# Turning the next batch's split queries and keys by DMA instead of on TensorE, and starting batch 1's attention inside round 0

## What is computed

```python
x = x + rnn(x, cond);  x = x + lstm(x, cond)        # both a scan over the tokens
x = x + hyperbolic_transformer(x, cond)
x = x + mixture_of_experts(x, cond)

# hyperbolic_transformer
xm = expmap0(layer_norm(logmap0(x)) * (1 + sc) + sh)
q, k, v = (to_heads(plin(xm, w, b)) for w, b in ...)        # 16 heads of 16
attn = softmax(logmap0(q) @ logmap0(k).T / 4);  o = expmap0(attn @ logmap0(v))
x1 = mobius_add(x, expmap0(g * logmap0(plin(from_heads(o), w_o, b_o))))   # first sum
ff = plin(plin(norm(x1), w_f1, b_f1), w_f2, b_f2)
return mobius_add(x1, expmap0(g2 * logmap0(ff)))                          # second sum

# mixture_of_experts: gate = softmax(means(x) @ gate_w ...), the best 2 of 4 experts per batch
y = sum_e w_e * mask_e * (gelu(x @ ew1_e + eb1_e) @ ew2_e + eb2_e) + gelu(x @ sw1 + sb1) @ sw2 + sb2
```

## Time and profile before

| | |
|---|---|
| median of 3 runs | 2327.17 us |
| profiled execution, its own time | 2326.94 us |
| its span, first to last instruction | 2325.2 us |
| TensorE matmul busy | 2204.3 us (95%) |
| VectorE busy | 1580.7 us (68%) |
| ScalarE busy | 1258.4 us (54%) |
| GpSimd busy | 560.5 us (24%) |
| mean granted TensorE clock | 0.993 |

### The profile page before, as it was taken

The page is one execution under the profiler, slowest core; times in us unless marked ns, Lnnn a source line. Parts: engine busy times, 40 slices in busy tenths (PEclk is TensorE's granted clock), DMA queues, the critical chain, the costliest instruction groups (busy, mean ns, idle before and its releaser), DMA issues. The chain is left out here.

```text
span 2325.2 us, 94850 instructions
## 1 busy us (share of the span) xinstructions
PE 2204.3 (95%) x39004; PEld 1452.3 (62%) x39004; DVE 1580.7 (68%) x7316; ACT 1258.4 (54%) x4381; POOL 560.5 (24%) x1178
## 2 busy tenths in 40 slices
PE   8899999999999999999988699999999999999999
PEld 6677777777777777777743256464646556464666
DVE  5777777777777777777757685765747476674520
ACT  4555555555555555555565665657565564656432
POOL 0222222242222422224223031222213131221100
PEclk9999999999999999999999799999999999999999
DMA  4111111101001000010010110303030020302020
GB/s 120 36 38 32 38 40 34 45 25 32 29 22 36 23 27 26 23 36 20 22 70 1 53 70 1 132 1 132 1 132 1 30 103 1 132 1 105 0 87 9
DMA packets 51874, 102.64 MB, mean 44 GB/s; under 512 B 10468, under 2 KB 33380, under 8 KB 47348
## 3 DMA queue, kind: packets, MB, share of 16 engines
q1 hardware_dynamic: 48036, 94.06, 11.8%
q10 hardware_dynamic: 3408, 2.52, 0.4%
HBM read 75.53 MB, written 21.04 MB: 42 GB/s over the span
## 5 line engine op out<-in xcount | busy, mean ns | idle before, releaser
L135 PE MATMUL psFI<-wh,Hs 128*8 128x128 f32 (+3 forms) x8192 | 324.7, 276 | 60.4 <-DVE Hs L250 47.2
L135 PE MATMUL psOR<-wh,RH 128*16 128x128 f32 (+3 forms) x8320 | 321.4, 272 | 2.0 <-ACT RH L338 2.0
L135 PEld LDWEIGHTS psFI<-wh,Hs 128*8 128x8 f32 (+3 forms) x8192 | 182.4, 99 | 178.6 <-DVE Hs L250 178.6
L2054 ACT ACTIVATE pexp<-bank 128x1024 f32<-128x1024 f32 x256 | 244.3, 1023 | 35.3 <-PE bank L1384 35.1
L338 ACT ACTIVATE RH<-RT 128x16 f32<-128x16 f32 x512 | 110.8, 216 | 261.3 <-DVE RT L254 261.3
L1262 PE MATMUL bank<-x3T,ew 128*128 128x512 f32 x512 | 238.7, 593 | 0.0
L234 DVE STREAM_TRANSPOSE FIT<-psFI 128x128 f32<-128x128 f32 x512 | 162.0, 316 | 101.4 <-PE psFI L135 98.8
L329 ACT ACTIVATE sFI<-FIT 128x32 f32<-128x32 f32 x512 | 118.6, 232 | 200.7 <-DVE FIT L234 195.7
L135 PEld LDWEIGHTS psOR<-wh,RH 128*16 128x16 f32 (+1 forms) x8320 | 205.7, 104 | 4.4 <-ACT RH L338 3.7
L135 PE MATMUL psG<-wh,Hs 128*8 128x64 f32 (+3 forms) x8192 | 208.3, 219 | 0.0
L1276 PE MATMUL bank<-ew,hidden 128*128 128x256 f32 x864 | 201.0, 379 | 0.0
(11 more groups left out here) (366 smaller groups left out, 4225.9 us busy)
## 6 DMA issues: line engine op xcount, KB each, us to landing
ew<-in_ew SPq DMA_DIRECT2D x32, 1024.0 KB, 9.2
qkv_scratch<-qkvr SPq DMA_DIRECT2D x31, 384.0 KB, 2.8
big<-qkv_scratch SPq DMA_DIRECT2D x7, 1536.0 KB, 7.9
XX<-in_xT SPq DMA_DIRECT2D x31, 256.0 KB, 2.8
x_scratch<-xr SPq DMA_DIRECT2D x32, 128.5 KB, 2.3
x<-x_scratch SPq DMA_DIRECT2D x8, 514.0 KB, 9.6
ada<-ada_scratch SPq DMA_DIRECT2D x8, 512.0 KB, 8.6
out_x<-x SPq DMA_DIRECT2D x7, 512.0 KB, 3.3
```

Source lines behind the costliest of these rows:

```text
L135: last = pe.matmul(bank[32 * j:32 * j + width, :], state(k), weights[:, k, j, cols], start=False, stop=k == KC - 1, tile_position=(0, 32 * ...
L2054: up(act.activation(M.pexp[:, n % 2, 2 * pr:2 * pr + 2, :], M.PS[pr][:, :, :], ACT.Exp, scale=1.0 / math.sqrt(HD)), "exps")
```

## The change

The 64 transposes on TensorE and the 8 copies are removed in all of rounds 0 to 6. SP issues instead 8 DMA transposes a round, each of 128 partitions x 1024 fp16 (256 KB), `spl` to `splT`, tile by tile as the low parts come; they stand behind the expert weight loads and ahead of the store. `scores(0)` of the next batch waits for all 8 (`splT_in`) and for the four `ff_bias`. VectorE's low parts move up between the linear outputs. In round 0 TensorE goes on after the linear layer with the first `AHEAD` = 3 units of batch 1 and the scores of the fourth, and ScalarE's exponentials of these units stand ahead of the squares of the second sum, ahead of its tanh and ahead of `mobius_scaled`. Round 1 begins at unit 3; its x is turned after `values(3)`, its gate steps stand two units later (logits before unit 6, `l_exp` after unit 8, factors still before unit 9). Squares of round 0 are thrown into `x3T` and `x3` instead of `pexp`, and the table of the exponential is loaded earlier in round 0. The two extra matmuls that kept TensorE busy at the end of round 0 go.

```diff
@@ Stage.SIGNALS
-        "splT_ps": 8, "scores": 32, "av": 16, "O_ps": 4, "tT_ps": KC, "wo_ps": 1,
+        ... "out": 16, "splT_in": 2 * NQ * 16,
+        "scores": 32, "av": 16, "O_ps": 4, "tT_ps": KC, "wo_ps": 1,
@@ tensor_round
-    def split_transposes(a, batch):
-        ...
-    def scores(n):
+    def scores(n, batch=b):
         ...
-            elif pr == 0 and b:
-                pe.wait_ge(*M.of_heads("splT_B", b))
-                pe.wait_ge(*M.of_heads("splT_A", b))
+            elif pr == 0 and batch:
+                pe.wait_ge(*M.of_heads("splT_in", batch))
+                pe.wait_ge(*at("ff_bias", batch - 1))
...
     def back(g, tiles=range(NQ)):
         pe.wait_ge(*at("oT", b, g + 1))
+        if g == 0 and b == 1:
+            pe.wait_ge(*at("x3T_lo", e))
...
     if front:
-        scores(0)
-        if experts and not e:
-            transposes(M.x1, (4, 5), "x3T_ps", "x_out", e)
+        if b != 1:
+            scores(0)
         for n, (g, kc) in enumerate(units):
+            if b == 1 and n < AHEAD:
+                continue
             ...
-            if n == 4 and experts:
+            if n == (4 if e else 6) and experts:
             ...
             values(n)
+            if b == 1 and n == AHEAD:
+                transposes(M.x1, (6, 7), "x3T_ps", "x_out", e)
...
         if experts:
-            steps(FC + LEAD + 4, STEPS - 3)
-        if b + 1 < NB:
-            split_transposes(0, b + 1)
-        if experts:
-            steps(STEPS - 3, STEPS - 1)
-        if b + 1 < NB:
-            split_transposes(1, b + 1)
-        if not experts:
-            pe.wait_ge(*at("pq", b, 2))
-            kept_busy(2)
-        if experts:
-            steps(STEPS - 1, STEPS)
+            steps(FC + LEAD + 4, STEPS)
+        else:
+            scores(0, b + 1)
+            for n in range(AHEAD):
+                scores(n + 1, b + 1)
+                values(n, b + 1)
@@ vector_round
     if experts and front:
+        if b == 1:
+            oT_moved(0)
         gate_logits(7)
...
         for q in range(NQ):
+            if heads and q < 2:
+                low_parts(b + 1, 2 * q)
+                low_parts(b + 1, 2 * q + 1)
             linear_outputs(q)
...
         mobius_factors(M.norm2.X2, 1)
-        if heads:
-            for q in range(NQ):
-                low_parts(b + 1, q)
         mobius_sum(1)
...
-        if heads:
-            for a, hp2 in SPLIT_B:
-                splT_moved(b + 1, a, hp2)
@@ scalar_round
+    def exponentials(n, batch=b):
+        for pr in range(2):
+            act.wait_ge(*at("scores", batch, 2 * n + pr + 1))
+            ...
-    if front and b:
+    if front and b > 1:
         act.activation(M.exp_scratch[:, :], M.mhalf[:, 0:1], ACT.Exp)
     ...
     if front:
-        for n in range(H // 4 * NQ):
-            ...
-            if n == 0 and experts and not e:
+        for n in range(AHEAD if b == 1 else 0, H // 4 * NQ):
+            exponentials(n)
+            if b == 1 and n == AHEAD + 1:
                 x3T_moved()
-            if n == 6 and experts:
+            if n == (6 if e else 8) and experts:
...
-            act.activation(M.exp_scratch[:, :], M.mhalf[:, 0:1], ACT.Gelu_apprx_tanh)
+            act.activation(M.exp_scratch[:, :], M.mhalf[:, 0:1], ACT.Gelu_apprx_tanh if experts else ACT.Exp)
...
         hidden(14)
+        if not experts:
+            exponentials(0, b + 1)
         mobius_squares(1, lambda: hidden(15))
         hidden(16)
+        if not experts:
+            exponentials(1, b + 1)
         tanh(1)
         hidden(17)
+        if not experts:
+            exponentials(2, b + 1)
         mobius_scaled(M.x1, 1)
         hidden(18)
         outputs(1)
-        hidden(19, 20)
-        if b + 1 < NB:
-            splT_moved(b + 1, (0, 0), (0, 2))
-        hidden(21, 22)
-        if b + 1 < NB:
-            splT_moved(b + 1, (1, 0))
-        hidden(23)
+        hidden(19, 20, 21, 22, 23)
@@ sync_round
+    if b + 1 < NB:
+        for q in range(NQ):
+            for a in range(2):
+                sp.wait_ge(*M.of_heads("lo", b + 1, 2 * q + a + 1))
+                sp.dma_start_transpose(M.splT[:, a, :, q * P:(q + 1) * P], M.spl[:, a, q].rearrange("p h s d -> p (h s d)")).then_inc(M.sem("splT_in"), 16)
```

More of the change, by code:

```diff
@@ L37 @@
 LEAD, HIDDEN, IN_NEXT = 3, 5, STEPS - 3
-SPLIT_ACT, SPLIT_B = [(0, 0), (0, 2), (1, 0)], [(0, 1), (0, 3), (1, 1), (1, 2), (1, 3)]
+AHEAD = 3
 class Signal:
@@ L1212, in place @@
         self.hsq = self.spl[:, :, :, :, :, :].rearrange("p a q h s d -> p (a q h s d)").bitcast(fp32)
+        self.dump_first = self.x3T[:, :, :].rearrange("p k t -> p (k t)"), self.x3[:, :, :].rearrange("p q d -> p (q d)")
         self.dump, self.dump_dve = self.pexp[:, 0, :, :].rearrange("p j (h d) -> p (j h) d", d=D), sb("dump_dve", [P, D])
@@ L1385, in scores, with values @@
             last.then_inc(M.sem("scores"), 1)
-    def values(n):
+    def values(n, batch=b):
         g, kc = units[n]
-        pe.wait_ge(*at("exps", b, 2 * n + 2))
+        pe.wait_ge(*at("exps", batch, 2 * n + 2))
         if n == 0:
-            if b:
-                pe.wait_ge(*M.of_heads("vt", b))
+            if batch:
+                pe.wait_ge(*M.of_heads("vt", batch))
             if experts:
@@ L1831, in vector_round @@
         dve.wait_ge(*at("x3T_ps", e, 2))
-        up(dve.tensor_copy(M.x3T[:, 1, :], bank(5)), "x3T_hi")
+        up(dve.tensor_copy(M.x3T[:, 1, :], bank(7 if b == 1 else 5)), "x3T_hi")
         gate_input()
@@ L1845, in vector_round @@
     if front:
-        oT_moved(0)
+        if b != 1:
+            oT_moved(0)
         if experts:
@@ L1974, in squares @@
     def squares(src, sums, where, q, raises=None):
-        ins = act.activation(M.dump[:, where + q, :], src[:, q, :], ACT.Square, accum_out=sums[:, q:q + 1])
+        dump = M.dump[:, where + q, :] if b else M.dump_first[where // 4][:, q * D:(q + 1) * D]
+        ins = act.activation(dump, src[:, q, :], ACT.Square, accum_out=sums[:, q:q + 1])
         if raises:
@@ L2020, in norm_squares @@
             squares(za, N.squares, 0, q, "squares2" if q == NQ - 1 else None)
[L2022 to L2026, removed]
-                up(act.copy(M.splT[:, a, 2 * hp2:2 * hp2 + 2, :].rearrange("p j t -> p (j t)"), bank(hp2).bitcast(fp16)), "splT_B" if (a, hp2) in SPLIT_B else "splT_A")
     def gram_moved(k):
@@ L2041, in x3T_moved @@
         act.wait_ge(*at("x3T_ps", e, 1))
-        up(act.copy(M.x3T[:, 0, :], bank(4)), "x3T_lo")
-    if front and b:
+        up(act.copy(M.x3T[:, 0, :], bank(6 if b == 1 else 4)), "x3T_lo")
+    def exponentials(n, batch=b):
+        for pr in range(2):
+            act.wait_ge(*at("scores", batch, 2 * n + pr + 1))
+            if n >= 2:
+                act.wait_ge(*at("av", batch, n - 1))
+            up(act.activation(M.pexp[:, n % 2, 2 * pr:2 * pr + 2, :], M.PS[pr][:, :, :], ACT.Exp, scale=1.0 / math.sqrt(HD)), "exps")
+    if front and b > 1:
         act.activation(M.exp_scratch[:, :], M.mhalf[:, 0:1], ACT.Exp)
@@ L2048, in scalar_round @@
     if front:
-        for n in range(H // 4 * NQ):
-            for pr in range(2):
-                act.wait_ge(*at("scores", b, 2 * n + pr + 1))
-                if n >= 2:
-                    act.wait_ge(*at("av", b, n - 1))
-                up(act.activation(M.pexp[:, n % 2, 2 * pr:2 * pr + 2, :], M.PS[pr][:, :, :], ACT.Exp, scale=1.0 / math.sqrt(HD)), "exps")
-            if n == 0 and experts and not e:
+        for n in range(AHEAD if b == 1 else 0, H // 4 * NQ):
+            exponentials(n)
+            if b == 1 and n == AHEAD + 1:
                 x3T_moved()
-            if n == 6 and experts:
+            if n == (6 if e else 8) and experts:
                 act.wait_ge(*at("l_max", e))
```

12 lines of the change are left out of this document (4 added, 8 removed).

## The result

The changed kernel takes 2295.68 us in the median of 4 runs (2295.32 to 2296.17) against 2327.06 us (2325.06 to 2328.14): a ratio of 0.9866, 95% interval 0.9851 to 0.9881, 31.4 us less. Its profiled execution took 2296.17 us with a span of 2294.3 us, 30.9 us under the span before. The forecast was 2303 us, in a range of 2293 to 2317.

The account below looks back on a forecast made before the run. TensorE was taken to bound the rounds with experts, a chain over VectorE, ScalarE and GpSimd round 0. Savings of 21.5 us (rounds 1 to 6) plus 2.7 (round 0) gave 2303 us, range 2293 to 2317.

Parts of the forecast that it names:

- the forecast's own case: Time per DMA transpose from 1.2 to 2.8 us, total 2299 to 2311 us, chance 0.61.
- d: Time per DMA transpose in a row of eight, taken as 1.75 us.
- 2289 + 8d: Forecast total in us, with d the time per DMA transpose; 2303 us as forecast.
- T: Time at which all 8 transposes of round 0 have landed, forecast 1301.2 us.
- The three conditions: Rounds 1 to 6: DMA lands in time, later second sum on VectorE harmless, ScalarE's 2.4 us push covered; 21.5 us saved.
- From T to unit 3: Round 0's transposes landed to start of attention unit 3 of batch 1: 12.8 us.
- units at the low clock: Batch 1's early attention units slowed by the clock round 0 left at 0.58: 1.5 us added.
- A new wait behind the gate: Round 1: biases start 5.6 us after the gate's factors, held by the bias loads: 2.5 us more.
- 1303.9 - T: Saving in round 0 and the start of round 1, up to the gapless expert steps: 2.7 us.
- rival 1: Fast transposes, at or below 1.2 us each; linear outputs and ScalarE's order set T: 2293 to 2299 us, chance 0.17.
- Rivals 2 and 3: Slow transposes stall round 0, 2327 us at 4.8, chance 0.13; block by block, rounds 1 to 6 too, about 2509, 0.09.
- rival 4: Rounds 1 to 6: ScalarE falls 2.4 us behind, TensorE waits up to 1 us each; 2309 us, no separate chance.

Follow-up runs that it names:

- low parts alone: Kernel before with only the low parts moved between the linear outputs, TensorE's transposes and copies kept: 2324.88 us.
- the doubled run: Changed kernel with a second DMA transpose into idle memory ahead of each of round 0's eight: 2308.24 us.
- the run with the gate earlier: Changed kernel with round 1's gate one unit earlier (logits before unit 5, its exponential after unit 7): 2295.65 us.
- the split wait: Changed kernel with the five transposes unit 0 needs issued first and waited for alone, the other three at unit 1: 2292.85 us.

## Why the prediction was right, and where it was off

The direction and the range held, and so did the mechanism of rounds 1 to 6: the transposes stood in a full TensorE, and their time came off. In round 0 the chain that was forecast is the one that the trace shows, but its terms were too large: 31.4 us came where 24.2 were forecast, and 2295.7 lies outside the 2299 to 2311 of the forecast's own case. With the measured pace, d = 1.38, "2289 + 8d" still gives 2300. The miss is 2.8 us in T, 2.7 us in the terms behind it and 1.1 us in rounds 1 to 6; where the remaining 0.6 us come from is open.

- *Rounds 1 to 6.* "2 x 1.79 = 3.58 us" was measured as 3.69 us a round, 22.1 instead of 21.5 us; one odd round before, of 132.4 us, and small differences make it 22.6. The 0.11 us more is the change between kinds of matmul at the two blocks' edges, which the chain gives to neither (this reading is argued). The three conditions held. The last transpose of all was issued at 2043.5 us, and the scores that need it follow the x turned at 2072.8 us, 29 us later; ScalarE's push cost nothing (rounds of 132.0 us in the run with low parts alone).
- *T, the term that was mis-sized.* The forecast had "1.32 plus the 0.33 to 0.45 us that SP needs to issue one, 1.75 us". But the issue is not added to a pace, it is as long as the pace. SP is busy 1.33 us with each transpose and starts the next 0.04 us later, and the last lands 3.3 us after its start. T was 1298.4 instead of 1301.2, 2.8 us of the miss. The doubled run shows that this term acts as the forecast had it, one for one. The chain through the last transpose of round 0:

```profile
1293.62 1.34 SPq L2196
1294.97 0.04 issue
1295.01 3.32 DMA splT<-spl
1298.33 0.04 issue
1298.38 0.62 PE bank L1369 x2
```

- *From T to the end of the squares*: 5.8 us, where 6.1 were forecast. *From T to unit 3*: 12.4 for 12.8.
- *A slip in the sum.* 12.8 + 14.1 + 0.9 is 27.8, and the forecast writes T + 28.1.
- *"I add 1.5 us for units at the low clock"*: not there. The factors stood at T + 27.8, the right sum without this term, not at T + 29.6. The clock was indeed 0.50 in the first units, but units 0, 1 and 2 began on ScalarE at 1299.0, 1304.0 and 1307.0, spaced by the steps of the sum, and a unit's matmuls at that clock are 1.04 + 1.93 = 3.0 us: they fitted in.
- *"A new wait behind the gate ... 2.5 us more"*: the place was right, size and cause were not. The biases came 4.8 us after the factors instead of 3.1, 1.7 more. What was late is VectorE's copy of the factors (1328.22, two us after the matmul), which stood behind the copy and squares of group 0 and the first copy of group 1. The wait for the bias loads that was named as a sign (some 2.5 us of VectorE) did not appear: they had landed by the time VectorE came to them, 5.9 us after the index at most, where I had 6.9. That they are the next limit is seen in the run with the gate earlier, where VectorE waited 0.26 us for one, until 6.2 us after the index.
- *Sum for round 0*: saving 1303.9 - T with T at 1298.4 would have been 5.5 us. 2.7 more came from behind T: 1.8 up to the factors, 0.9 at the wait behind the gate. 8.40 was measured by the head, 8.25 by the start of the gapless part.
- *The rivals.* The measured 2295.7 lies in the band of rival 1 (2293 to 2299), but not by its mechanism: T was not set by the linear outputs, and d was 1.38, above its 1.2. That its number came out all the same is luck: the terms behind T were forecast 2.7 us too large. Rivals 2 and 3 fall with the measured pace. For rival 4 no wait was found. What my list lacked is that the early start itself might be worth next to nothing: I priced it together with the low parts and never asked for the time without it.
- *The pages that the forecast names.* The trace has 256 KB per 1.38 us in a row of eight, 190 GB/s. The Trainium skill's "DMA: Bandwidth & Descriptors", section Latency and other measured facts, has an effective 261 GB/s; by estimate this is 1.0 us for the same and a saving of 8.7 us. The measured saving, 8.40, is close to it, but by two misses that cancel, since T was 3.2 us later than with that figure. The Trainium skill's "VectorE: DVE Perf Modes", section The three transpose paths, has 1309 ns for a 128x128 block. In the trace a whole transpose of eight such blocks takes about that, so as a pace the measurement goes against it.

## What to carry to other kernels

Before you price an early start, follow the engine that has to execute it in order: here ScalarE waited for the new work ahead of squares that could have run, and gave back what the early units brought. Put the wait behind the work that is already due, and let the work fill it. And price parts that enable each other together and one by one: here 2.7 and 0.9 us alone were 11.5 us together, and the third part added 0.6.

## What the runs showed of the hardware

- A DMA transpose holds SP for its whole pace, 1334 ns in the median of 56 (1259 to 2158). The plain DMAs right behind the first row took 0.33 to 0.53 us to issue. In the median over all rounds it was 0.33 us for the 4 KB biases, 0.33 and 0.48 us for the 1 MB expert weights, and 1.05 us for the `ada` loads.

```profile
L2196 SPq DMA_TRANSPOSE splT<-spl x56: 1259/1334/2158, 1285.3 to 2043.5; - x56
...
DMA to landing us min/median/max: 3.1/3.3/5.1
```

- Eight in a row are bound by the issuing, as far as the traces can tell. The DMA engines look full as well while a row runs (share 1.00 in the stretch below, last but one column). But SP is held for 1.26 to 1.37 us by the first of a row too, with no other transpose in flight, and in the doubled run the sixteenth lands 3.2 us after its start, the first 3.3: nothing piles up. And where a transpose was held up, as in round 1, the next ones landed only 0.74 and 0.86 us apart (1398.63, 1399.37, 1400.23), while SP issued every 1.38 us or more: the transfers can go faster than the queue issues them.

```profile
1521.80:1532.80 11.00, 11.00 (x35) 6.32 (x34) 9.68 (x30) 3.46 (x14) 1.02 (x1) 1.00 1.00 191
```

- A load of program instructions goes with late landings: the longest of a row is 3.5 us at most without one, and up to 5.4 us with one. This is shown under the split wait.
- DMA transposes move in small pieces: 111007 packets instead of 51874 for 14.6 MB more, 1056 a transpose, and all of the increase is in packets under 512 B.
- The rounds with experts did not feel the transposes: 128.33 us with eight in them, 128.34 in round 7 without.
